# A decoder's attention phase: one group's normalisation and reductions a slot earlier, and four extra products of constants on TensorE

## The reference

```
x = x + L0_attn(layernorm(x))          # a gated recurrence over 128 tokens
x = x + L0_xattn(layernorm(x), ctx)    # 16 heads of 64, 128 extra keys
x = x + L0_ffn(layernorm(x))           # top 2 of 8 experts
x = x + L1_attn(layernorm(x))          # 16 heads of 8, causal; q and k normalised per head
x = x + L1_xattn(layernorm(x), ctx)    # 16 heads of 8, window of 64 tokens
x = x + L1_ffn(layernorm(x))           # one product, inputs and weights rounded to 4 bits
```

```
q = (x @ Wq.T), k = (x @ Wk.T), v = (x @ Wv.T)      # 16 heads of 8
q = layernorm(q, gq, bq); k = layernorm(k, gk, bk)  # over the 8 channels of a head
out = softmax(causal(q k^T)) v ;  x = x + out @ Wo.T + bo
```

## Time and profile before

| what | value |
|---|---|
| median of three runs | 1635.24 us |
| the profiled execution's own time | 1637.81 us |
| its span, first to last instruction | 1636.1 us |
| PE busy | 1425.1 us, 87% |
| DVE busy | 1210.3 us, 74% |
| ACT busy | 1123.4 us, 69% |
| POOL busy | 578.7 us, 35% |
| mean granted TensorE clock | 0.963 of full |

### The profile page before, as it was taken

One profiled execution on the slowest core, in us unless ns is written; L12 is line 12 of the kernel. 1 busy time (PEld: TensorE's weight loads), 2 busy tenths in 40 slices (PEclk: granted clock), 3 DMA queues, 4 the chain that ended last, 5 costly groups with the idle time before them and its releaser, 6 DMA issues. The chain is left out here.

```text
span 1636.1 us, 42886 instructions
## 1 busy us (share of the span) xinstructions
PE 1425.1 (87%) x15385; PEld 1058.7 (65%) x15385; DVE 1210.3 (74%) x2848; ACT 1123.4 (69%) x2842; POOL 578.7 (35%) x623
## 2 busy tenths in 40 slices
PE   2358999999999999999974999777899999999995
PEld 0125777777777767677763888645667677776663
DVE  3999789898988887765545555467678898887665
ACT  1127998888888888798852556445667767767652
POOL 0011424343524343314014100155446656444452
PEclk9999999999999999999995999869999999999997
DMA  6733231423232121100121222230000110000000
GB/s 173 163 94 77 52 85 47 106 51 87 58 79 69 49 73 46 66 21 13 61 65 50 61 58 61 59 83 18 8 23 10 37 36 10 22 21 2 22 9 14
DMA packets 78012, 87.56 MB, mean 54 GB/s; under 512 B 11120, under 2 KB 67312, under 8 KB 73328
## 3 DMA queue, kind: packets, MB, share of 16 engines
q1 hardware_dynamic: 70192, 72.58, 17.6%
q0 software_dynamic: 4096, 8.40, 1.8%
q10 hardware_dynamic: 3520, 3.84, 0.7%
HBM read 66.97 MB, written 17.83 MB: 52 GB/s over the span
## 5 line engine op out<-in xcount | busy, mean ns | idle before, releaser
L893 ACT ACTIVATE pr<-P,nm 128x256 f32<-128x256 f32 x512 | 237.8, 490 | 4.1 <-DVE nm L1043 4.0
L1943 ACT ACTIVATE et<-P 128x1024 f32<-128x1024 f32 x128 | 131.3, 1026 | 106.0 <-PE P L1730 105.6
L1043 DVE TENSOR_REDUCE nm<-P 128x4 f32<-128x1024 f32 x128 | 156.5, 1222 | 59.2 <-PE P L694 53.6
L324 POOL TENSOR_TENSOR rstd<-ve,mhalf 128x1 f32<-128x1 f32 (+2 forms) x83 | 76.9, 928 | 245.9 <-DVE ve L319 245.0
L877 ACT COPY ptS<-P 128x512 f32<-128x512 f32 x256 | 136.8, 585 | 32.9 <-PE P L708 28.2
L708 PE MATMUL P<-ident,pr 128*128 128x128 f32 x1024 | 140.1, 280 | 9.5 <-issue 7.2
L868 ACT ACTIVATE pr<-pr,ri 128x256 f32<-128x256 f32 x256 | 118.8, 522 | 33.9 <-DVE pr L1034 33.2
L692 PE MATMUL P<-kt_w,qt_b 64*128 64x128 f32 x1024 | 127.1, 309 | 3.2 <-ACT pr L893 2.7
L708 PEld LDWEIGHTS P<-ident,pr 128*128 128x128 f32 x1024 | 110.3, 142 | 26.2 <-issue 13.8
L2103 DVE TENSOR_REDUCE qS<-P 128x8 f32<-128x1024 f32 x64 | 78.4, 1226 | 56.4 <-PE P L1723 55.4
L607 POOL TENSOR_TENSOR kv_w<-kv_w,r_w1h 128x512 f32<-128x512 f32 x48 | 61.1, 1273 | 164.2 <-DVE pr L1034 164.2
(11 more groups left out here) (325 smaller groups left out, 4138.8 us busy)
## 6 DMA issues: line engine op xcount, KB each, us to landing
kv_w<-scr_v SPq DMA_DIRECT2D x16, 1024.0 KB, 8.0
r_w1h<-scr_r SPq DMA_DIRECT2D x16, 1024.0 KB, 10.8
xt<-scr_xs SPq DMA_DIRECT2D x71, 64.0 KB, 1.8
scr_ys<-yt SPq DMA_DIRECT2D x71, 64.0 KB, 1.5
x<-in_x SPq DMA_DIRECT2D x8, 256.0 KB, 9.4
scr_v<-mixing SPq DMA_DIRECT2D x8, 256.0 KB, 2.0
scr_r<-mixing SPq DMA_DIRECT2D x8, 256.0 KB, 2.1
xb<-in_x SPq DMA_DIRECT2D x8, 256.0 KB, 4.5
```

Source lines behind the costliest of these rows:

```text
L324: nc.gpsimd.tensor_tensor(rstd[:, k, lo:hi], ve[:, k, lo:hi], mhalf[:, lo:hi], ALU.pow).then_inc(S[rs_sem], 1)
L893: e = nc.scalar.activation(pr[:, s % 3, h * KEYS:(h + 1) * KEYS], scores(s)[:, h // 2, (h % 2) * KEYS:(h % 2 + 1) * KEYS], ACT.Exp, bias=n ...
L1043: nc.vector.tensor_reduce(nm[:, s % 3, 0:4].rearrange("p (a h) -> p a h", a=2), scores(s).rearrange("p a (h k) -> p a h k", k=KEYS), AX.X, ...
L1943: nc.scalar.activation(et[:, u % 4, :, :, :], scoresT, ACT.Exp).then_inc(S["h_exp"], 1)
```

## The change

Group 1's steps from `nm` to `kt1` are one slot earlier (`qt1` and all after it stay), its `nmr` is made at the end of slot 1's vector work by a new step `nm_late` and no longer in slot 2, and the second and third part of group 0's inverse roots are earlier by up to two slots. A helper `fill` multiplies the identity with the query-key-value weights `wD` into PSUM bank 5 (which nothing reads before the first product with values writes it): twice behind the first keys' and queries' transposes (slot -5), once behind the scores in slots 0 and 1.

```diff
+        "qp": None, "nm_late": None, "kt0": -13, ...
     1: {...
-        "sum0": -1, "sum1": 0, "sum2": 1, "sum3": 1, "stat0": 1, "stat1": 1, "nm": 2, "xn0": 2, "xn1": 2,
-        "dxt": 3, "bias": 7, ... "qp": 4, "square": 4, "v": 5,
-        "reduce": 5, "guess": 5, "inv0": 5, "inv1": 6, "inv2": 6, "kn": 6, "qn": 6,
-        "kt0": 7, "qt0": 7, "kt1": 8, "qt1": 8, "kt2": 9, "qt2": 11, "kt3": 12, "qt3": 13},
+        "sum0": -1, "sum1": 0, "sum2": 1, "sum3": 1, "stat0": 1, "stat1": 1, "nm": None, "nm_late": 1, "xn0": 1, "xn1": 1,
+        "dxt": 2, "bias": 7, ... "qp": 3, "square": 3, "v": 4,
+        "reduce": 4, "guess": 4, "inv0": 4, "inv1": 5, "inv2": 5, "kn": 5, "qn": 5,
+        "kt0": 6, "qt0": 6, "kt1": 7, "qt1": 8, "kt2": 9, "qt2": 11, "kt3": 12, "qt3": 13},
 PART_AT = ({...},
-           {"square": -8, "reduce": -3, "guess": -3, "inv0": -3, "inv1": -2, "inv2": -2, "kn": -2, "qn": -2},
-           {"square": -2, "reduce": 0, "guess": 0, "inv0": 0, "inv1": 0, "inv2": 1, "kn": 1, "qn": 1})
+           {"square": -8, "reduce": -5, "guess": -5, "inv0": -5, "inv1": -3, "inv2": -3, "kn": -3, "qn": -3},
+           {"square": -2, "reduce": -1, "guess": -1, "inv0": 0, "inv1": 0, "inv2": 0, "kn": 0, "qn": 0})
 # tensor_program
+                def fill(n):
+                    for _ in range(n):
+                        nc.tensor.matmul(P[:, 5, 0:384], ident[:, :], wD[:, :], start=True, stop=True)
 # behind the scores of a slot
+                    if s in (0, 1):
+                        fill(1)
 # behind kt0 and the first queries' transposes, slot -5
+                                if b == 0:
+                                    fill(2)
 # vector_program, behind the statistics of a slot
+                    g = self_at(s, "nm_late")
+                    if g is not None:
+                        ln_shift(dve, 0, 0, GS, "d_rs", norms(g), "d_nm")
```

## The result

The changed kernel takes 1639.03 us (median of 20 runs, 1637.19 to 1641.21) against 1635.55 us before (20 runs). The ratio is 1.0016, with a 95% interval of 1.0009 to 1.0023. A gain of 1.5 us was forecast; the loss is 1.5 to 3.8 us by the interval. The time lies within the stated range, and within the band of 0.5%, but on the other side. The profiled execution took 1639.85 us.

The account below looks back on a forecast made before the run. PE was taken as nearest to full, with DVE busier in slots 5 to 7. Unit 8 +0.5 and the ladder -2.0 gave -1.5 us: 1635.2 to 1633.7, rounded 1634; range 1628.5 to 1640.

Parts of the forecast that it names:

- DVE up to `ve`: Slots -1 to 1: DVE runs without holes from 1077.1, ending group 1's statistics at 1088.6 instead of 1089.92; gain 1.3 us.
- the wait for POOL's power: Slot 1: DVE stands for POOL's power of 1.04 us, until 1089.9, with unit 2's maxima queued behind it.
- `xnD` ahead of the exponentials: ACT starts the four `xnD` at 1089.95 instead of 1094.12, now before unit 0's exponentials.
- The added products cost next to nothing in slot -5: Two products behind the first transposes cost 0 to 1.3 us; 0.1 taken, including a late copy's 0.1.
- the clock hardly matters in slots 0 to 2: Unit 1's scores end at 1084.6 at the low clock, DVE is free at 1084.4; the high clock wins 0.2 us.
- The loss in slots 2 and 3: `dxt` ahead of `kt3` in bank 7 makes unit 3 3.4 us late, 2.1 at high clock; unit 5's scores 1.7 late.
- rival 2: Chance 0.25: bank 7 sets the pace, slower by 3.0 us, 1638.2, if DVE finishes group 1's `qn` after 1119.
- `qp` 2.83 with mixed clock [...], here 1.8: Slot 3: the queries' products take 1.8 us instead of 2.83, as PE is busy from 1094 on.
- So I keep both blocks: Slots 4 and 5: two DVE passes blocked beside POOL's select and gathers stay, each 1.85 us instead of 0.25.
- The ladder's gain: Sequence 0's keys' and queries' ladder moves to slot 6, taking waits and transposes from slot 8; 2.4 us less, 2.0 counted.
- What follows is mostly PE's [...] and keeps the difference.: Behind slot 8, work is mostly PE's (87% busy over the span), so the -1.5 us stays to the end.
- rival 1: Chance 0.18: holes inside units 3 and 4 and two blocked DVE passes don't recur; -6.9 us, 1628.3.

Follow-up runs that it names:

- e3: Changed kernel with `kt3` of group 0 in slot 1 instead of 2; ratio to the kernel before 1.0002 (1615.73 against 1615.26 us).
- e9: The kernel before, unchanged, profiled a second time; one execution, 1639.30 us.
- e5: The changed kernel itself, measured again on another chip; ratio to the kernel before 1.0019 (1618.59 against 1615.52 us).
- e12: Changed kernel with group 0's bias on GpSimd in slot 2 instead of 4; ratio to the kernel before 1.0009 (1638.20 against 1637.17 us).
- e8: Kernel before with GpSimd relieved: group 4's first two gathers moved to slot 12, group 2's bias to 13; ratio to the kernel before 0.9999.
- e7: Changed kernel with `kt3` in slot 1, group 4's first two gathers in slot 12 and group 2's bias in 13; ratio to the kernel before 0.9985.
- e4: Changed kernel with group 0's bias on GpSimd in slot 3 instead of 4; ratio to the kernel before 1.0011 (1617.38 against 1615.26 us).

## Why the prediction was wrong

- **DVE up to `ve`, the wait for POOL's power, `xnD` ahead of the exponentials: right.** Forecast 1088.6, 1089.9, 1089.95 and 1093.8 for the end of the `xTd` copy; seen, with 0.95 added for the earlier phase, 1089.0, 1090.3, 1090.4 and 1093.9.
- **The added products cost next to nothing in slot -5: right**, 0.4 us where 0.1 was taken and 1.3 the bound. That the clock hardly matters in slots 0 to 2 was right as well: the stage had 0.88 of full clock and DVE still set unit 2.
- **The loss in slots 2 and 3: right in place and in size.** 3.4 us forecast for unit 3, 2.9 seen. The sum carried it, and rival 2's own sign, that DVE finishes `qn` after 1119, did not come: it finished at 1116.6, forecast 1117. But I had let the DVE chain behind it start 1.9 us earlier all the same (rival 2's "against"), and weighed the loss as repaid. Moving `kt3` away gives 2.7 to 3.7 us of time back, so all of it goes through to the end; without it the new order is level with the kernel before (e3).
- **"`qp` 2.83 with mixed clock [...], here 1.8" and "values' products 0.6": a gain that the order doesn't make.** The first trace alone had the low clock there (2.83 and 1.08 us). The three other traces of the old order have 1.89 and 0.64 to 0.65, so some 1.4 us of the forecast's gain was the baseline trace's bad luck, and without it the sum comes to about 0 (my estimate from these rows).
- **"So I keep both blocks": mis-sized.** One of the two is 3.06 us instead of 1.85, as group 0's bias is not moved and now falls behind the select of the same slot. The holes between halves of units 3 and 4, which I kept at 1.21 and 1.1, were none and 0.45 in this trace, so that the two errors nearly cancel: unit 7's maxima ended at 1123.2 both by the forecast and in the trace (1122.28 and 0.95). That agreement is luck.
- **The ladder's gain: right in kind**, 3.2 us between units 7 and 9 (12.02 before, 8.85 after), 2.5 against e9; 2.0 forecast.
- **The step that failed: "What follows is mostly PE's [...] and keeps the difference."** It doesn't. Slots 8 and 9 became short (3.5 us each in e5), and GpSimd, whose gathers, selects and bias are listed by slot, did not fit into them. In four traces it holds PE by a select and DVE by a long pass, for 1.7 us and more; in two others PE stood for ACT's `qm` copy. With GpSimd relieved no trace of the new order loses anything there.

In the two first traces the sum is -1.0 at unit 9, +3.2 between units 9 and 12, +0.8 in the last stretch behind unit 127: 3.0, less 0.95 of earlier start, makes the 2.0 of the two spans. The +0.8 is not the change's: that stretch took 36.0 to 36.1 us in ten of the fourteen traces and 36.8 to 37.1 in the other four, of which e9, the kernel before, is one. The medians are 1.4 us further apart than the spans, which is within the scatter of single executions. The terms above are single traces' sizes and don't add up to the ratio one by one. What the times show are the two moves: 2.7 to 3.7 us for `kt3`, and 1.8 to 2.7, likely but with intervals that overlap, for GpSimd. A slip of the prediction's ranges: rival 1's end, 1628.3, lies just outside the 1628.5 that was to take it in.

What stays open: why ACT's `qm` copy in slot 10 stood 1.38 us in the trace after and 1.31 in e12 with nothing in the profile to wait for, and the holes between halves of units; e9 has them again (1.09 and 1.01 us), e8 on its chip has none.

## What to carry to other kernels

When steps of a written-out order move a slot earlier, list for each slot what every engine has in it, also the one that is "only 35% busy": slots that get shorter must still hold the gathers, masks and additions pinned to them. A step that takes turns in a shared PSUM bank must not be put ahead of one that the next unit's path needs. Test a moved order by relieving one suspect in both the old and the new order; only what helps the new one alone explains the difference. And take a second trace of the kernel before, ahead of the sum: a low-clock spell in the first one looks like a gain to be had.

## What the hardware showed that I had not expected

- A pass of VectorE between SBUF tensors that meets GpSimd doesn't wait for one instruction of it but for a run: 3.06 us over gather, select and bias (0.96, 1.10, 1.28 us back to back), 3.15 us in slot 10, for a pass of 0.23 to 0.35 us. The Trainium skill, "SBUF — State Buffer", section "SBUF: two separate sides", has the loser blocked for the other's whole instruction; these traces show a whole run. The same passes kept their length away from such a run, and also in the first moments of a gather: in e9 the first pass behind the reduction began 0.18 us into one and took 0.23 us, and the next, 0.45 us into it, took 1.71. The maxima, which read PSUM, took 1.21 to 1.23 us in all fourteen traces.
- The clock of one and the same kernel falls at different places from run to run: the queries' products (8 records) took 2.83 us in the first trace of the kernel before and 1.89 in the second, and in the new order 1.89, 2.61 (e7) and 3.42 (e4). One trace's gain of a microsecond there is no result.
